# Edge counts of a graph adjacency matrix: one mask and two comparisons for four chunks of edges in place of two comparisons for each chunk

## The chip, the cores and the metric

The kernel runs on one core of a Trainium2 chip. The metric is the device time of one execution in microseconds (us), as the median of several executions. TensorE multiplies matrices, VectorE, ScalarE and GpSimd work elementwise, and SyncE issues DMAs. Each engine has a queue (a sequencer) that also executes register, branch and semaphore instructions in order and hands the others to the engine's data path.

## The reference, cut to what matters

A graph has 3125 nodes with 256 features and 100000 edges, sorted by destination. The destinations are `3125 * uniform ** 2`, so that low node numbers have many edges and high ones few. A chain of graph layers follows: four GCN layers, a graph-attention branch beside a state-space (Mamba) branch, three relational layers over eight edge types, and a last attention layer.

```python
x = normal(3125, 256); src = randint(100000, 0, 3125)
dst = minimum((3125 * uniform(100000) ** 2.0).astype(int32), 49999)
src, dst = both in the stable order of argsort(dst)
agg = segment_sum(norm[:, None] * h[src], dst)        # GCN
attn = exp_e / (segment_sum(exp_e, dst)[dst] + 1e-16)  # attention
```

The kernel works for GCN and attention from a dense matrix: entry (s, d) is the number of edges from node s to node d. The change is in the stage that makes this matrix.

## The kernel before

Nodes are padded to 3200, 25 tiles of 128. The edges are cut into 782 chunks of 128, one edge on each partition. The program runs stage by stage, with a barrier of all engines between stages: `constants`, `edge_tables`, `adjacency`, `load_x`, and then the layers.

`edge_tables` (lines 125 to 267) loads sources, destinations and types, turns them on TensorE so that a chunk is a column, and makes two keys for each edge: `key_lo`, which is (destination / 16) * 128 + source % 128, and `key_hi`, which is 16 * (source / 128) + destination % 16. It sends the smallest and largest destination of every chunk through DRAM, and works out for each of 200 groups of 16 destinations the first chunk that touches it, how many chunks do, and how many steps come before.

`adjacency` (lines 285 to 461) makes the matrix column by column. For each group n, VectorE walks over its chunks (line 321). For each chunk it writes `low` (128 x 128, line 325), which is 1 where the edge belongs to the group and its source modulo 128 is the column, and `high` (128 x 400, line 327), which is 1 at the column of its source tile and its destination in the group. TensorE multiplies the two (line 357) and accumulates the group's 128 x 400 counts in one of four PSUM banks. A ring of four slots (`RING`) lies between the engines: VectorE waits on `s_used`, TensorE on `s_hot`. The first chunk's product opens the bank (`start=True`), a product with zeros closes it (line 364), and ScalarE copies it to `counts` (line 416). After eight groups a tile is complete: ScalarE casts it (line 424), and in the next tile's groups 1 to 5 TensorE turns it (line 370, 25 products) and sums degrees (lines 375 and 377, 25 and 8 products), while ScalarE writes a mask of absent edges (line 407) and SyncE stores counts, cast strip and mask. A group has at least two steps, so that the first can stand outside the loop.

At each group, VectorE's and TensorE's queues call `group_of` (line 2489), which loads two registers from `g.groups`, one of them holding two numbers that are taken apart by `% 1024` and `// 1024`. `span_of` (line 270) is the like of it for the relational layers, with three loads.

## Time and profile before

| | |
|---|---|
| median of 3 executions | 9598.99 us (9585.42 to 9602.02) |
| the profiled execution, its time | 9601.42 us |
| its span in the trace | 9599.7 us |
| adjacency, first comparison to last product | 59.3 to 1396.5 us |
| steps in it, groups in it | 984, 200 |

A page of the profile shows the busy time of each engine, the span in 40 equal slices (here 240 us each) in tenths, the DMA queues and the costliest groups of instructions. Queries of the trace give the same for a stretch, a line or a tile, the waits, and the instructions in order of time. Names such as DVE are the engines': PE is TensorE's products, PEld its weight loads, DVE VectorE, ACT ScalarE, POOL GpSimd, SPq SyncE's queue; a q behind any name means the queue. Idle time put down to "issue" is time in which the data path waited for nothing but its own queue.

### The profile page before, as it was taken

The page shows a single profiled execution, that of the slowest core. Times are in us where ns is not written, and L with a number is a line of the kernel's source. Part 1 is how long each engine was busy: PE and PEld are TensorE (multiplying, and loading weights), DVE is VectorE, ACT ScalarE, POOL GpSimd, SP SyncE. Part 2 cuts the span into 40 slices and gives each one's busy share as a digit, 9 for nine tenths or more (in the row PEclk, how much of TensorE's full clock was granted, in tenths as well). Part 3 has the DMA queues.
Part 4 walks back from the last instruction along what each step waited for, and adds up shares of the span by engine and source line. Part 5 has one row for each costly group of instructions (what it writes and reads, how often), then busy time and mean ns, then how long its engine had stood idle before and what let it go on. Part 6 is the DMA issues. An engine that isn't in the chain of part 4 may idle for free. (4 is left out here: it accounts for less than half of the span.)

```text
span 9599.7 us, 112171 instructions
## 1 busy us (share of the span) xinstructions
PE 5887.8 (61%) x17649; PEld 2850.3 (30%) x17651; DVE 5067.8 (53%) x10613; ACT 1592.7 (17%) x2777; POOL 4423.1 (46%) x3713
## 2 busy tenths in 40 slices
PE   3444446621666633334489889888898888850453
PEld 1111116510222211113343444434444334430111
DVE  5443335659999958982333322233322333327896
ACT  0112221100444422112300000100011000010342
POOL 0000000030677716761027766576765777740793
PEclk5555557765899956667795677756777556665897
DMA  0112235532222220002243444433444333343333
GB/s 18 41 59 78 72 116 204 202 135 86 87 73 72 74 82 1 1 28 81 85 156 105 121 124 130 135 105 118 125 131 129 106 108 111 112 124 105 115 105 103
DMA packets 566945, 951.06 MB, mean 99 GB/s; under 512 B 78123, under 2 KB 441492, under 8 KB 564472
## 3 DMA queue, kind: packets, MB, share of 16 engines
q1 hardware_dynamic: 358280, 480.94, 15.7%
q0 software_dynamic: 142720, 403.03, 14.2%
q10 hardware_dynamic: 65888, 66.44, 2.1%
q8 instruction: 22, 0.36, 0.0%
q14 instruction: 35, 0.29, 0.0%
HBM read 718.07 MB, written 232.06 MB: 99 GB/s over the span
## 5 line engine op out<-in xcount | busy, mean ns | idle before, releaser
L2263 POOL DMA_INDIRECT rel1s_rows<-rel_table,rel1s_at x876 | 829.6, 947 | 393.5 <-DVE rel1s_at L2249 221.7
L2263 POOL DMA_INDIRECT rel0s_rows<-rel_table,rel0s_at x876 | 829.1, 946 | 370.6 <-DVE rel0s_at L2249 194.5
L2278 PE MATMUL rel2s_acc<-rel2s_rows,rel2s_hot 128*128 128x256 f32 x1752 | 879.7, 617 | 158.3 <-DMA rel2s_rows<-rel_table,rel2s_at 87.6
L2263 POOL DMA_INDIRECT rel2s_rows<-rel_table,rel2s_at x876 | 830.4, 948 | 302.4 <-issue 124.8
L357 PE MATMUL adj_acc<-adj_high,adj_low 128*128 x984 | 474.4, 487 | 711.3 <-DVE adj_high L327 706.2
L1371 PE MATMUL gatx_acc<-gatx_w,gatx_feat 128*65 128x400 f32 x1600 | 664.7, 569 | 338.3 <-DVE gatx_w L1293 296.2
L2278 PE MATMUL rel0s_acc<-rel0s_rows,rel0s_hot 128*128 128x256 f32 x1752 | 784.1, 565 | 127.0 <-DMA rel0s_rows<-rel_table,rel0s_at 72.1
L2278 PE MATMUL rel1s_acc<-rel1s_rows,rel1s_hot 128*128 128x256 f32 x1752 | 773.2, 557 | 135.0 <-DMA rel1s_rows<-rel_table,rel1s_at 78.1
L1283 DVE SCALAR_TENSOR_TENSOR gatx_w<-gatx_t,gatx_s 128x400 f32 (+1 forms) x800 | 745.9, 990 | 1.2 <-ACT gatx_t L1324 1.2
L325 DVE TENSOR_SCALAR adj_low<-g_numbers,g_offsets,g_key_lo 128x128 f16 x984 | 309.6, 315 | 801.7 <-issue 793.9
L1033 POOL IOTA rankk_owni<- 128x25 int32 x1 | 0.2, 159 | 1435.6 <-POOLq L72 1435.6
L1391 POOL TENSOR_SCALAR gatx_w<-gatx_w 128x400 f32<-128x400 f32 (+1 forms) x200 | 431.0, 2155 | 457.8 <-ACT gatx_w L1330 457.8
L2251 DVE TENSOR_SCALAR rel0s_hot<-g_numbers,g_dsts 128x128 f32 x876 | 290.5, 332 | 648.2 <-PE rel0s_acc L2278 630.6
L2251 DVE TENSOR_SCALAR rel1s_hot<-g_numbers,g_dsts 128x128 f32 x876 | 290.4, 332 | 643.3 <-PE rel1s_acc L2278 625.5
L2251 DVE TENSOR_SCALAR rel2s_hot<-g_numbers,g_dsts 128x128 f32 x876 | 297.7, 342 | 605.9 <-PE rel2s_acc L2278 599.5
L2278 PEld LDWEIGHTS rel2s_acc<-rel2s_rows,rel2s_hot 128*128 128x128 f32 x1752 | 412.6, 282 | 621.5 <-DVE rel2s_hot L2251 310.8
L2278 PEld LDWEIGHTS rel0s_acc<-rel0s_rows,rel0s_hot 128*128 128x128 f32 x1752 | 381.4, 258 | 521.8 <-DVE rel0s_hot L2251 231.1
L2278 PEld LDWEIGHTS rel1s_acc<-rel1s_rows,rel1s_hot 128*128 128x128 f32 x1752 | 376.0, 254 | 523.8 <-DVE rel1s_hot L2251 250.4
L1330 ACT ACTIVATE gatx_w<-gatx_w,gatx_s 128x400 f32<-128x400 f32 x800 | 437.1, 617 | 519.4 <-DVE gatx_w L1283 519.4
L1371 PE MATMUL latx_acc<-latx_w,latx_feat 128*65 128x400 f32 x800 | 307.4, 507 | 267.0 <-POOL latx_w L1393 267.0
L1846 PE MATMUL mamb_acc<-mamb_hc,g_ident 128*128 128x512 f32 x420 | 237.0, 731 | 381.6 <-DVE mamb_hc L1837 381.6
L1371 PEld LDWEIGHTS gatx_acc<-gatx_w,gatx_feat 128*65 128x65 f32 x1600 | 234.1, 155 | 765.5 <-DVE gatx_w L1293 411.7
(478 smaller groups left out, 9670.1 us busy)
## 6 DMA issues: line engine op xcount, KB each, us to landing
agg_strip<-strips SPq DMA_DIRECT2D x100, 800.0 KB, 6.0
adj<-adj_counts SPq DMA_DIRECT2D x25, 1600.0 KB, 7.1
gatx_adj<-adj SPq DMA_DIRECT2D x200, 200.0 KB, 2.4
latx_adj<-adj SPq DMA_DIRECT2D x200, 200.0 KB, 2.3
gatx_feat<-local_rows SPq DMA_DIRECT2D x200, 130.0 KB, 2.3
rel_table<-rel0p_res POOLq DMA_DIRECT2D x25, 1024.0 KB, 5.1
rel_table<-rel0s_prod ACTq DMA_DIRECT2D x25, 1024.0 KB, 4.9
rel_table<-rel1s_prod ACTq DMA_DIRECT2D x25, 1024.0 KB, 5.0
```

Of the source, the lines that this page charges most:

```text
L325: nc.vector.tensor_scalar(low[:, bass.ds(slot, 1), :].rearrange("p a d -> p (a d)"), base[:, 0:P], g.offsets[:, bass.ds(n, 1)], g.key_lo[: ...
L357: nc.tensor.matmul(bank[:, 0:W16], low[:, bass.ds(slot, 1), :].rearrange("p a d -> p (a d)"), high[:, bass.ds(slot, 1), :].rearrange("p a ...
L1033: nc.gpsimd.iota(owni[:, :], [[P, T]], base=-HALF, channel_multiplier=1).then_inc(s_io, 1)
L1283: last = nc.vector.scalar_tensor_tensor(w[u][:, h, :], t1[:, h, bass.ds(c, J)], s08[:, bass.ds(s, 1), h], t2[:, h, bass.ds(c, J)], ALU.add ...
L1330: last = nc.scalar.activation(w[u][:, h, :], w[u][:, h, :], ACT.Exp, bias=s02[:, bass.ds(s, 1), h])
L1371: last = nc.tensor.matmul(acc[k][h][:, :], feat[u][:, h * 65:(h + 1) * 65], w[u][:, h, :], start=False, stop=False)
L1391: nc.gpsimd.tensor_scalar(mine, mine, 1.0, None, ALU.min).then_inc(s_pm, 1)
L1846: last = nc.tensor.matmul(acc[:, a:b], ident[:, :], hc[:, a:b], start=False, stop=False)
L2251: nc.vector.tensor_scalar(hot[u][:, :], g.numbers[:, bass.ds(t * P, P)], g.dsts[:, bass.ds(c0 + u, 1)], None, ALU.is_equal).then_inc(s_hot, 1)
L2263: pool.indirect_dma_start(rows[u][:, :], None, table, bass.IndirectOffsetOnAxis(ap=at[u][:, 0:1], axis=0)).then_inc(s_in[u], 16)
L2278: nc.tensor.matmul(acc[:, :], hot[u][:, :], rows[u][:, :], start=False, stop=False).then_inc(s_used, 1)
```

## The change

Four chunks make one step, a batch (`Q = 4`), and a group has one batch or more. The constants hold every number four times in a row, so that the four chunks of a batch are the innermost dimension of one instruction. Each edge now has three 16-bit keys: source modulo 128 (`key_lo`), the column of `high` plus 1 (`key_hi`), and the destination group (`key_group`). In a batch VectorE makes `mine` (128 x 4), which is `key_hi` where the edge is of this group and 0 elsewhere, then `low` for four chunks (128 x 128 x 4) and, after a wait for `mine`, `high` for four chunks (128 x 400 x 4), both by TENSOR_TENSOR. TensorE makes four products from operands whose elements stand four apart. The ring has two slots of a batch in place of four of a chunk. A bank is opened by a product with zeros. The three numbers of a group lie side by side, and one load instruction brings them into three registers; they need no division. `edge_tables` takes the keys from the turned numbers with integer operations, and turns three arrays, not four. `spans` gets the same layout, but `span_of` keeps its three loads.

```diff
-RING = 4
+RING = 2
+Q = 4
@@ edge_tables, VectorE
-            nc.vector.tensor_scalar(bits[:, 0], raw[:, 1], 3, ~(P - 1), ALU.logical_shift_left, ALU.bitwise_and)
...
-            nc.vector.tensor_tensor(keys[:, 0], bits[:, 0], bits[:, 1], ALU.add)
-            nc.vector.tensor_tensor(keys[:, 1], bits[:, 2], bits[:, 3], ALU.add)
+            dve.wait_ge(s_T, 3)
+            nc.vector.tensor_copy(ints[:, 0, :], psum[0][:, 0:W])
+            v(nc.vector.tensor_copy(ints[:, 1, :], psum[1][:, 0:W]))
...
+            nc.vector.tensor_copy(g.key_lo[:, :], bits[:, 0, :])
+            nc.vector.scalar_tensor_tensor(g.key_hi[:, :], bits[:, 1, :], 1.0, bits[:, 2, :], ALU.add, ALU.add)
+            nc.vector.tensor_copy(g.key_group[:, :], bits[:, 3, :])
...
-            nc.vector.tensor_scalar(count, count, 2.0, None, ALU.max)
+            whole(count, Q)
@@ adjacency, VectorE
+            dve.wait_ge(s_io, 1)
+            nc.vector.tensor_copy(num1[:, :, :], numi[:, :, :])
+            nc.vector.tensor_scalar(num0[:, :, :], numi[:, 0:P, :], -1.0, None, ALU.add).then_inc(s_num, 1)
+            dve.wait_ge(s_num, 1)
                 with dve.Fori(0, count, 1) as j:
-                    c = step_start(nc, first + j)
+                    c = step_start(nc, first + j * Q)
                     slot = dve.snap((before + j) % RING)
                     dve.wait_ge(s_used, before + j + 1)
-                    nc.vector.tensor_scalar(low[:, bass.ds(slot, 1), :].rearrange("p a d -> p (a d)"), base[:, 0:P],
-                                            g.offsets[:, bass.ds(n, 1)], g.key_lo[:, bass.ds(c, 1)], ALU.add, ALU.is_equal)
-                    nc.vector.tensor_scalar(high[:, bass.ds(slot, 1), :].rearrange("p a d -> p (a d)"), base,
-                                            g.key_hi[:, bass.ds(c, 1)], None, ALU.is_equal).then_inc(s_hot, 1)
+                    nc.vector.scalar_tensor_tensor(slot_of(mine, slot).rearrange("p a q -> p (a q)"), g.key_group[:, bass.ds(c, Q)],
+                                                   g.group_number[:, bass.ds(n, 1)], g.key_hi[:, bass.ds(c, Q)],
+                                                   ALU.is_equal, ALU.mult).then_inc(s_mine, 1)
+                    nc.vector.tensor_tensor(slot_of(low, slot).rearrange("p a n q -> p (a n) q"), num0[:, :, :],
+                                            g.key_lo[:, bass.ds(c, Q)].unsqueeze(1).to_broadcast([P, P, Q]), ALU.is_equal)
+                    dve.wait_ge(s_mine, before + j + 1)
+                    nc.vector.tensor_tensor(slot_of(high, slot).rearrange("p a n q -> p (a n) q"), num1[:, :, :],
+                                            slot_of(mine, slot).to_broadcast([P, W16, Q]), ALU.is_equal).then_inc(s_hot, 1)
@@ adjacency, GpSimd
+            nc.gpsimd.iota(numi[:, :, :], [[1, W16], [0, Q]], base=1, channel_multiplier=0).then_inc(s_io, 1)
@@ adjacency, TensorE
-                pe.wait_ge(s_copied, n + 1)
-                visit(0, True)
-                with pe.Fori(1, count, 1) as j:
-                    visit(j, False)
+                pe.wait_ge(s_copied, n + 1)
+                nc.tensor.matmul(bank[:, 0:W16], g.zeros[:, 0:P], g.zeros[:, 0:W16], start=True, stop=False)
+                with pe.Fori(0, count, 1) as j:
+                    slot = pe.snap((before + j) % RING)
+                    pe.wait_ge(s_hot, before + j + 1)
+                    for i in range(Q):
+                        last = nc.tensor.matmul(bank[:, 0:W16], low[:, bass.ds(slot, 1), :, i].rearrange("p a n -> p (a n)"),
+                                                high[:, bass.ds(slot, 1), :, i].rearrange("p a n -> p (a n)"),
+                                                start=False, stop=False)
+                    last.then_inc(s_used, 1)
@@ three registers in one load
+def three_of(nc, eng, table, n, regs, least, most, last):
+    eng.reg_load(regs, table[0:1, bass.ds(n, 1), :].rearrange("o n k -> o (n k)"))
+    first, count, before = (eng.snap(r) for r in regs)
...
-    both = eng.value_load(g.groups[0:1, 0, bass.ds(n, 1)], min_val=2 * 1024, max_val=C * 1024 + C - 1)
-    before = eng.value_load(g.groups[0:1, 1, bass.ds(n, 1)], min_val=0, max_val=NG * C)
-    return both % 1024, eng.snap(both // 1024), before
+    return three_of(nc, eng, g.groups, n, regs, 1, most, NG * most)
```

## Rows read from the trace of the kernel before

**Rows 1.** The page: the span in 40 slices of 240 us.
```profile
PEclk5555557765899956667795677756777556665897
...
GB/s 18 41 59 78 72 116 204 202 135 86 87 73 72 74 82 1 1 28 81 85 156 105 121 124 130 135 105 118 125 131 129 106 108 111 112 124 105 115 105 103
```

**Rows 2.** Stretch: length; busy PE, PEld, DVE, ACT, POOL; clock, DMA share, GB/s.
```profile
112.90:1399.00 1286.10, 599.84 (x2520) 216.64 (x2518) 506.43 (x1854) 255.41 (x321) 0.00 (x0) 0.52 0.18 61
```

**Rows 3.** Waits from 57 to 1408 us: total, times, longest.
```profile
DVE adj_low L325 <- issue: 793.9, 964, 3.7
PE adj_acc L357 <- DVE adj_high L327: 706.2, 914, 3.7
...
DVE adj_low L325 <- PE adj_acc L357: 7.8, 20, 0.4
```

**Rows 4.** VectorE in order of time: start, duration; two steps and a group's end between.
```profile
1101.81 0.32 DVE L325 TENSOR_SCALAR adj_low<-g_numbers,g_offsets,g_key_lo 128x128 f16 x1 [0.39 <-issue]
...
1104.69 0.32 DVE L325 TENSOR_SCALAR adj_low<-g_numbers,g_offsets,g_key_lo 128x128 f16 x1 [2.33 <-issue]
...
1105.63 0.32 DVE L325 TENSOR_SCALAR adj_low<-g_numbers,g_offsets,g_key_lo 128x128 f16 x1 [0.40 <-issue]
```

**Rows 5.** VectorE's queue by line: duration in ns, minimum, median, maximum.
```profile
L325 DVEq FUSED_REGOPS  x1968: 62/118/230, 58.9 to 1395.2; - x197
...
L2492 DVEq FUSED_REGOPS  x400: 65/130/190, 58.0 to 1393.6; - x134
...
L2492 DVEq TENSOR_LOAD <-g_groups x200: 299/303/992, 58.1 to 1393.2; - x100
```

**Rows 6.** TensorE's queue: weight loads in order of time, then instructions by line.
```profile
1391.72 0.15 PEld L357 LDWEIGHTS adj_acc<-adj_high,adj_low 128*128 x1 [0.18 <-issue]
...
1392.32 0.10 PEld L357 LDWEIGHTS adj_acc<-adj_high,adj_low 128*128 x1 [0.45 <-issue]
...
L2491 PEldq FUSED_REGOPS  x380: 42/157/171, 57.5 to 1393.1; - x190
...
L2491 PEldq TENSOR_LOAD <-g_groups x200: 296/303/976, 57.0 to 1392.8; - x100
...
L357 PEldq ALU_OP  x984: 32/36/36, 60.1 to 1396.1; - x197
```

**Rows 7.** TensorE in order of time: turning, and the two degree sums.
```profile
1388.77 0.81 PE L375 MATMUL adj_ind<-g_ones,adj_strip 128*128 128x1 bf16 x25
...
1389.43 2.83 PE L377 MATMUL adj_deg<-adj_strip,g_ident 128*128 128x400 bf16 x8
...
1400.09 1.89 PE L370 MATMUL adj_tp<-g_ident,adj_strip 128*128 128x128 bf16 x16 [3.47 <-ACT adj_strip L424]
```

**Rows 8.** Two VectorE lines with one tensor input: minimum, median, maximum ns.
```profile
L120 DVE CAST g_numbers<-const_num x1: 1827/1827/1827, 5.5 to 5.5; 128x3200 f16<-128x3200 int32 x1
...
L1073 DVE TENSOR_SCALAR rank_before<-g_numbers,rank_own x25: 1046/1053/1055, 1529.8 to 1833.2; 128x3200 bf16<-128x3200 f16 x25
```

**Rows 9.** The stages before adjacency, in order of time.
```profile
2.43 2.80 POOL L114 IOTA const_num<- 128x3200 int32 x1
...
21.14 1.09 DVE L221 TENSOR_TENSOR edge_keys<-edge_bits 128x896 f32<-128x896 int32 x1
22.15 1.08 DVE L222 TENSOR_TENSOR edge_keys<-edge_bits 128x896 f32<-128x896 int32 x1
...
24.68 0.27 DVE L227 COPY edge_endsT<-edge_t 14x128 f32<-14x128 f32 x1
...
31.95 0.63 DVE L236 TENSOR_SCALAR edge_tmp<-edge_row,edge_edge 100x782 f32<-100x782 f32 x1 [0.70 <-DMA edge_row<-ends_rows]
...
55.92 0.16 DVE L266 CAST g_spans<-edge_tiles 1x25 int32<-1x25 f32 x1
56.00 0.16 DVE L267 CAST g_spans<-edge_tiles 1x25 int32<-1x25 f32 x1
```

More of the change, by code:

```diff
@@ L264, in _ @@
-            nc.vector.tensor_tensor(g.spans[:, 2, 0:T], total_t, steps_t, ALU.subtract)
-            nc.vector.scalar_tensor_tensor(g.groups[:, 0, :], count, 1024.0, first, ALU.mult, ALU.add)
-            nc.vector.tensor_copy(g.spans[:, 0, 0:T], first_t)
-            nc.vector.tensor_copy(g.spans[:, 1, 0:T], steps_t)
+            nc.vector.tensor_copy(g.groups[:, :, 0], first)
+            nc.vector.tensor_copy(g.groups[:, :, 1], count)
+            nc.vector.tensor_tensor(g.groups[:, :, 2], total, count, ALU.subtract)
@@ L270, in span_of @@
+            nc.vector.tensor_copy(g.spans[:, :, 0], first_t)
+            nc.vector.tensor_copy(g.spans[:, :, 1], steps_t)
+            nc.vector.tensor_tensor(g.spans[:, :, 2], total_t, steps_t, ALU.subtract)
 def span_of(eng, g, t, size):
-    k, K = SPANS.index(size), len(SPANS)
     most = -(-C // size)
-    first = eng.value_load(g.spans[0:1, 0, bass.ds(t, 1)], min_val=0, max_val=C - 1)
-    count = eng.value_load(g.spans[0:1, 1 + k, bass.ds(t, 1)], min_val=2 if size == G_SUM else 1, max_val=most)
@@ L276, in span_of @@
-    before = eng.value_load(g.spans[0:1, 1 + K + k, bass.ds(t, 1)], min_val=0, max_val=T * most)
+    first = eng.value_load(g.spans[0:1, bass.ds(t, 1), 0], min_val=0, max_val=C - 1)
+    count = eng.value_load(g.spans[0:1, bass.ds(t, 1), 1], min_val=LEAST, max_val=most)
+    before = eng.value_load(g.spans[0:1, bass.ds(t, 1), 2], min_val=0, max_val=T * most)
     return first, count, before
@@ L345, in _ @@
             pe.sem_inc(s_used, RING)
+            regs = three_registers(pe, "group")
             pe.sem_inc(s_copied, 4)
@@ L2486, in row_number, with three_registers, group_of @@
     return nc.vector.scalar_tensor_tensor(out, kind, float(NP), src, ALU.mult, ALU.add)
[L2489 to L2493 removed]
+def three_registers(eng, name):
+    return [eng.alloc_register(f"{name}{k}") for k in range(3)]
+def three_of(nc, eng, table, n, regs, least, most, last):
+    eng.reg_load(regs, table[0:1, bass.ds(n, 1), :].rearrange("o n k -> o (n k)"))
+    why = "made by edge_tables within these bounds"
+    first, count, before = (eng.snap(r) for r in regs)
+    return (nc.s_assert_within(first, 0, C - 1, skip_runtime_bounds_check_because=why),
+            nc.s_assert_within(count, least, most, skip_runtime_bounds_check_because=why),
+            nc.s_assert_within(before, 0, last, skip_runtime_bounds_check_because=why))
+def group_of(nc, eng, g, n, regs):
+    most = -(-C // Q)
+    return three_of(nc, eng, g.groups, n, regs, 1, most, NG * most)
 def program(nc, x, src, dst, kind, noise, gcn, local, ssm, mix, rel, last, out):
```

129 lines of the change are left out of this document (64 added, 65 removed).

## The prediction

> **What bounds the kernel now.** The page comes first. The program runs stage by stage, and the stage that changes, adjacency, fills the first five and a half slices, with TensorE's clock granted at 0.5 and DMA far below what later slices move [rows 1]. The busy times of the stretch say that no data path is the bound there: TensorE is busy 600 of 1286 us, VectorE 506, ScalarE 255, DMA 18% [rows 2]. The waits say who holds up whom. TensorE waits 706 us for `adj_high`, 914 times; VectorE waits for TensorE 20 times, 7.8 us in all; and VectorE's own idle time, 794 us, is put down to its queue [rows 3]. VectorE in order of time gives the prices. A step lasts 0.94 us, though its two comparisons end 0.55 us after the first begins; where a group ends, the next step starts 2.88 us after the last, so a group costs 1.94 us beside its steps [rows 4]. With 984 steps and 200 groups that is 984 x 0.94 + 200 x 1.94 = 1313 us, and the stage measures 1337 us (59.3 to 1396.5), 2% more. So the stage is bound by register and branch work in VectorE's queue. Every later stage stands behind the barrier at its end, and what the stage gains comes off the span whole.
>
> **How many steps are left.** I took the chunks that each group touches from the reference's sorted destinations. The sum of max(2, chunks) over 200 groups is 984, the count in the trace; the sum of ceil(chunks / 4) is 299. There are 135 groups of one batch, 52 of two and 13 of three to 15. So 200 first batches come with a group's cost and 99 without. Four per batch is almost nowhere full: 1196 products replace 984, since short groups multiply empty chunks.
>
> **VectorE's queue.** A batch has the old step's work and one instruction more, with register addresses for `mine`, `key_group` and `key_hi`, and one more wait. The nearest rows are the register instructions of line 325, 0.118 us each [rows 5]; two of these with their gaps make 0.36, so 1.30 us for a batch. Bounds: 0.94 (nothing more) and 1.5. A group loses one load (0.303), two register instructions (0.130 each) and the division, with gaps some 0.8 of its 1.94 us [rows 5], and gains three copies between registers; I take 1.25, between 1.1 and 1.45. First batches: 200 x 2.55 = 510 us.
>
> **VectorE's data path.** No row shows a TENSOR_TENSOR with only 16-bit operands. The 4-byte one of 896 elements starts 1.01 us before its successor, that is 0.93 at one element a cycle of 1.04 ns and 0.08 more [rows 9]. For one input, going from a 4-byte to a 2-byte source takes 3200 elements from 1.83 to 1.05 us [rows 8]. I apply that halving: `low` (512) 0.35, `high` (1600) 0.91, `mine` 0.08 like the small instructions that start 0.08 apart [rows 9]. That is 1.34, with 0.1 for the wait 1.45 us, longer than the queue's 1.30, and it sets the 99 further batches: 144 us. In first batches it lies beside the queue's 2.55 us. VectorE together: 510 + 144 = 654 us. If the halving does not hold, the batch is 0.08 + 0.61 + 1.75 = 2.44 us, and with the wait 2.54: 200 x 2.6 + 99 x 2.54 = 771 us. The Trainium skill ("VectorE: DVE Perf Modes", "The perf-mode tier table") says that tensor_tensor runs at two elements a cycle for 16-bit data in SBUF and at one for fp32; by it the sum is the 654, and by the 4-byte row alone the 771; no run here shows yet which.
>
> **TensorE's data path.** Eight 400-column products last 2.83 us, of which a product's own tail is counted once: 0.333 us each at the granted 0.5 [rows 2, 7]. 1196 of them are 398 us; 200 openers with zeros 67; 200 closers some 20; and for each of 25 tiles the turning (25 of which 16 last 1.89 us, so 2.95) and the degree sums (0.81 and 2.83), 6.6 us, are 165 [rows 7]. Together 650 us. Opening by zeros costs 67 us of data path and takes a bank's start out of the loop; before, TensorE was waiting anyway.
>
> **TensorE's queue.** Two steps whose inputs were ready stand 0.60 us apart [rows 6]. Three more products add address arithmetic (two register instructions of 0.032) and dispatch; with gaps 0.23 each, between 0.15 and 0.33. Batch: 1.3 us (1.05 to 1.6). A group had two loads at 0.303 with some 0.16 of register work and a check after each [rows 6], about 1.7 us; one less leaves 1.1 with opener and closer. 299 x 1.3 + 200 x 1.1 + 25 x 2.4 for the tile's other instructions = 669 us.
>
> **The sum.** 654, 650 and 669 us are three resources of one load, joined by two slots. In most tiles eight groups take 21 us on each, but TensorE's comes in lumps (3.6 us of degree sums in one group, longer than a group's 2.55 us). Before, with the others half idle, the excess over the sum was 2%; I take 12% over the largest: 750 us. 1337 - 750 = 587 us less.
>
> **Around it.** In `edge_tables` four bit operations and two sums leave the path ahead of `edge_ends` going to DRAM (that transfer holds the spans from 24.68 to 31.95 us [rows 9]); the transfer starts some 4 us earlier, but two copies, the bit operations and three key instructions now stand before the spans on VectorE, some 8 us from the turned numbers on: 1 us earlier in all. `whole` adds three dependent instructions, and the layouts two: 1 us later. In adjacency, the iota of 1600 numbers (half of the 2.80 us of line 114 [rows 9]) and two casts (half of 1.83 [rows 8] and less) come before the first batch: 3 us. Net 3 us. `span_of` keeps three loads in 75 tiles, where only an address changes: 0, at most 2 us. Stores: 82 MB in 750 us are 109 GB/s, against 204 in a later slice [rows 1], so they stay hidden; without that cover a tile would wait for the store two before it. ScalarE's 255 us hide in 750.
>
> The profiled execution took 9601.4 us; 9601.4 - 587 + 3 = 9017, and the median stands 2.4 below it: **9015 us**.
>
> **Rivals.**
> - *VectorE at one element a cycle* (13%). 771 us and 8% for handover, 830 us: 9095. For it: no row with two 16-bit tensors; against: the halving in [rows 8]. A broadcast operand with rows of four elements could also prevent it.
> - *Dearer queues* (15%). Every strided slice gets its own address arithmetic: 1.6 us a batch and 1.3 a group on TensorE, 478 + 260 + 60 = 798, with 6% 845: 9110. For it: queues, not data paths, set the pace before [rows 3].
> - *A faster clock* (8%). With TensorE busy 85% and not 47% [rows 2], 2.4 GHz might be granted; the later stages with a clock of 0.8 and more are in [rows 1]. Then the queues decide: 690 us, 8955.
> - *The ring serialises* (4%). If two slots let no work overlap, 654 + 650 = 1304 us: 9569. Against: VectorE needs a slot only two batches later.
> - *TensorE reads at half speed* (7%). Both operands now have a stride of four elements. At 0.667 us a product: 798 + 252 = 1050, with 12% 1180 us: 9445.
> - *TensorE reads at a quarter* (3%), the one on the other side. 1196 x 1.333 + 252 = 1846 us, 509 more: 10111. It decides from (1337 - 252) / 1196 = 0.91 us a product on. Every TensorE row of before reads whole runs, the degree sums runs of 16 elements [rows 7], so nothing excludes it. The Trainium skill ("Advanced Engine Details and Errata", "Memory Cachelines") says that SBUF gives full performance from two hits on a 16-byte line and less where each access opens another; four fp16 numbers apart are exactly two hits, so by it nothing is lost here, and with eight chunks in a batch it would be; no run here shows it.
>
> **How the numbers follow.** The forecast has 50%, the rivals 13, 15, 8, 4, 7 and 3. The low end is the queues' sum with no excess at a fast clock, 640 us (8905). The high end takes the slow comparison and the dear queues together, 905 us (9170). In between lie the forecast and three rivals, 86%. A measurement here tells a change from none at 0.2%, 19 us: faster 0.95, within 0.01, slower 0.04.
>
> **What would show it.** In the changed profile: 299 of `adj_high`; `high` at 0.9 to 1.1 us (at 1.8 the halving failed); successive further batches 1.45 us apart; 2.55 us between groups of one batch; products 0.333 us apart in fours (wider: the stride, or the queue if the data path idles between). VectorE's wait for TensorE should grow from 7.8 us to the order of 100. Wrong would be: a product over 0.4 us, first batches over 3 us apart, or a stage after adjacency whose length changes.

## The result, and the profile after

The changed kernel takes 10330.93 us, median of 4 executions (10314.73 to 10334.56), against 9597.4 us for the kernel before (4 executions, 9585.42 to 9602.02). The ratio is 1.0763 (1.0744 to 1.0782). It is 733 us slower, where 9015 us and a gain of 587 us were forecast. The prediction has the wrong sign, and its range (8905 to 9170) does not hold the time.

Three parts of the page of the changed kernel: the slices, now of 258 us, two DMA queues (packets, MB, share), and two groups of products.

```profile
span 10332.9 us, 111704 instructions
...
PEclk7875567777657988566698667776677656665797
...
GB/s 43 105 136 158 137 128 134 133 133 143 122 99 86 73 73 70 71 1 1 64 59 152 117 115 127 130 133 105 117 127 131 119 107 109 112 120 119 108 105 103
...
q1 hardware_dynamic: 372680, 562.87, 16.8%
...
q10 hardware_dynamic: 146528, 125.42, 3.9%
...
L675 PE MATMUL agg_acc<-agg_split,agg_strip 128*128 128x192 bf16 (+1 forms) x5000 | 648.4, 307 | 472.8 <-DMA agg_strip<-strips 472.7
...
L379 PE MATMUL adj_acc<-adj_high,adj_low 128*128 x1196 | 462.9, 531 | 53.9 <-DVE adj_high L342 41.1
```

The slices show two things. The clock in the first three is 0.7 to 0.8, where it was 0.5 [rows 1], and the two slices of over 200 GB/s that stood behind adjacency [rows 1] are gone: six slices of 128 to 143 GB/s, the fifth to the tenth, stand in their place. The last two rows name the two kinds of products. The 1196 of adjacency are there as forecast. The 5000 of line 675 are the aggregation of the GCN layers, which no line of the diff touches, and they waited 472.7 us for strips from DRAM.

Stretches of the changed kernel (columns as in [rows 2]): adjacency, `load_x`, and the aggregation.

```profile
65.00:836.00 771.00, 633.53 (x2986) 271.25 (x2987) 451.13 (x896) 250.72 (x319) 0.00 (x0) 0.77 0.29 102
848.00:1310.00 462.00, 21.01 (x626) 18.70 (x626) 228.25 (x133) 1.51 (x2) 0.16 (x1) 0.50 0.49 147
1390.00:2600.00 1210.00, 660.71 (x5213) 605.76 (x5214) 262.03 (x135) 35.64 (x104) 0.00 (x0) 0.77 0.39 137
```

Adjacency is nearly as short as forecast: 771 us, where 750 were forecast, against 1337. The loss comes behind it. Two single lines show it: the instructions of one line, with count, duration in ns (minimum, median, maximum) and first and last start. First the changed kernel.

```profile
L805 DVE TENSOR_TENSOR loadx_low<-loadx_counts,loadx_high x25: 3491/3493/3493, 871.8 to 1300.0; 128x3200 bf16<-128x3200 f32 x25
...
L675 PE MATMUL agg_acc<-agg_split,agg_strip x5000: 245/296/373, 1396.8 to 2587.1; 128*128 128x192 bf16 x97, 128*128 128x195 bf16 x96
its engine sat idle before it (us, times) until:
  DMA agg_strip<-strips: 968.9, 201
```

The same two in the kernel before, whose lines 786 and 656 they are.

```profile
L786 DVE TENSOR_TENSOR loadx_low<-loadx_counts,loadx_high x1: 3493/3493/3493, 1432.1 to 1432.1; 128x3200 bf16<-128x3200 f32 x1
...
L656 PE MATMUL agg_acc<-agg_split,agg_strip x2500: 245/247/373, 1531.9 to 1845.3; 128*128 128x192 bf16 x97, 128*128 128x195 bf16 x96
its engine sat idle before it (us, times) until:
  issue: 0.7, 4
```

The counts are what matters here, not the durations: 25 rounds in place of 1, and 5000 products in place of 2500. A round or a product is the same instruction as before. The 968.9 us of waiting are those of the products and of their weight loads together; the products' own are the 472.7 of the page. Twice the products take 3.8 times as long (1190.3 us against 313.4). One wait of SyncE's queue, which issues the loads of strips, says why (total, times, longest):

```profile
SPq L657 <- PE agg_acc L675: 908.7, 100, 16.0
```

Both strips of a tile go to the same buffer, one after the other. SyncE issues loads in order and waits at each second strip until TensorE is through with the first, 100 times and 908.7 us in all; a strip then needs 4.5 us (median) from issue to landing. With one strip a tile TensorE waited for none. No run changed the buffers, so this is read from the trace and the code. The whole difference can be added up from these starts:

| stretch | before | after | difference |
|---|---|---|---|
| start of the program to adjacency's last product | 1396.2 | 835.9 | -560 |
| last product to first `loadx_low` | 35.9 | 35.9 | 0 |
| first to last `loadx_low` | 0 | 428.2 | +428 |
| last `loadx_low` to first product of the aggregation | 99.8 | 96.8 | -3 |
| first to last product of the aggregation | 313.4 | 1190.3 | +877 |
| sum | | | +742 |

The spans differ by 10332.9 - 9599.7 = 733 us, so the later stages give 9 back.

What decides the counts stands at the end of `adjacency`, in lines that the diff only moves (349 to 356 after, 334 to 341 before); the waits between them and the semaphore counts are left out here:

```python
nc.vector.tensor_reduce(most[0:1, :], acc[0][0:1, 0:P], AX.X, ALU.max)
...
nc.vector.tensor_scalar(most[0:1, :], most[0:1, :], 256.0, 1.0, ALU.is_ge, ALU.add)
...
nc.vector.tensor_scalar(g.strips_before[:, :], g.numbers[0:1, 0:32], float(HALF), most[0:1, 0:1], ALU.add, ALU.mult)
nc.vector.tensor_scalar(g.low_tiles[:, :], most[0:1, 0:1], float(T - 1), float(T - 2), ALU.mult, ALU.subtract)
```

`most` is the largest out-degree of a node, as the matrix has it. From 256 on the kernel no longer relies on a bf16 number to hold a count exactly, and each tile gets a second strip with what the first may have lost: `low_tiles` goes from 1 to 25 rounds, and the aggregation takes two strips a tile. The 100000 edges are 781 chunks of 128 and 32 edges. The last chunk with edges is filled up with 96 padding edges from node 3199 to node 3199 (the `memset` of `raw` with `PAD`), and what lies beyond is padding alone. Before, the last group has one chunk with edges and takes the least number of steps, two: 96 + 128 = 224 padding edges on node 3199. After, its one batch reads four chunks: 96 + 3 * 128 = 480. That is over 256, and the program chooses the long way, though the entry (3199, 3199) belongs to no node of the graph.

### The profile page after: what moved, and what is told of

Same layout as the page of the kernel before. It is cut to its first block and busy times, and to the rows that moved or that the text cites. A ratio compares the mean times of both kernels' runs of the same rounds, so it can differ in the third digit from the quotient of the medians.

```text
span 10332.9 us, 111704 instructions
## 1 busy us (share of the span) xinstructions
PE 6338.5 (61%) x21155; PEld 3289.5 (32%) x21156; DVE 5166.5 (50%) x9671; ACT 1589.3 (15%) x2775; POOL 4431.7 (43%) x3714
## 5 line engine op out<-in xcount | busy, mean ns | idle before, releaser
L675 PE MATMUL agg_acc<-agg_split,agg_strip 128*128 128x192 bf16 (+1 forms) x5000 | 648.4, 307 | 472.8 <-DMA agg_strip<-strips 472.7
L675 PEld LDWEIGHTS agg_acc<-agg_split,agg_strip 128*128 128x128 bf16 x5000 | 579.1, 124 | 523.8 <-DMA agg_strip<-strips 496.2
```

Source lines behind the costliest of these rows:

```text
L675: last = nc.tensor.matmul(acc[u][:, 0:W], strip[u][:, s * P:(s + 1) * P], split[:, s, :], start=False, stop=False)
```

## Experiments

The theory (padding): the 480 padding edges set the second strip, and the rest of the change brings what was forecast. Its rival: the later stages are slower for something else that the change does to them, such as the layout of `spans`, the place of the strips or the clock. Once this was settled, the runs went to adjacency: which of its prices bounds it now.

Every kernel below that loads three numbers at once also holds them in registers of their own (three register instructions more in `three_of`, 0.07 us a group on VectorE's queue); this is not shown again. With it the last product of adjacency comes at 847.8, 849.9 and 846.4 us in experiments 1, 2 and 4, against 835.9 in the changed kernel. The kernel before took 10150.8 us on the chip of experiments 1 to 4, 10164.0 us on that of 5 to 8, and 9600.65 us on that of 9 to 12, so whole times are not compared across chips. Adjacency itself is compared by its last product: the kernel before has it at 1396.2 us on the chip of the prediction, and the same adjacency in experiment 3 at 1396.5 on the slower chip of experiments 1 to 4. The other two chips have no trace of it.

**1 and 2. The limit just at and just above 480.** Only the constant of the comparison is changed.

```diff
-            nc.vector.tensor_scalar(most[0:1, :], most[0:1, :], 256.0, 1.0, ALU.is_ge, ALU.add).then_inc(s_v, 1)
+            nc.vector.tensor_scalar(most[0:1, :], most[0:1, :], 480.0, 1.0, ALU.is_ge, ALU.add).then_inc(s_v, 1)
```

> The changed kernel; the comparison behind the stage takes two strips per tile from a largest out-degree of 480 on, where it took them from 256. Each of the three loaded numbers is also held at 0 or more by a register instruction, as in every later run on the changed kernel. Theory A (padding): a group's last batch reads up to three chunks past the 782 of the edge list, each 128 padding edges from node 3199 to node 3199, so that node's out-degree is 96 + 3 x 128 = 480 and the flag stays set: about 10330 us as the changed kernel, load_x with 25 rounds and 200 strip loads, and the register instructions worth 0 to 20 us. Theory B (the counts of real nodes are too high, for example a bank not cleared by its opener): also 10330 us, since whatever value crossed 256 may exceed 480. Theory C (the largest degree lies between 256 and 479 for another reason): one strip, about 9040 us.

> The changed kernel with the comparison from 481 on. Theory A: the largest out-degree is 480 exactly, so the flag is not set; load_x goes back to one round (32 us in place of 462) and the aggregations to 100 strip loads. What the changed kernel lost behind adjacency is its 733 us plus the 561 us that adjacency ended earlier, 1294 us; so 10331 - 1294 = 9037 us, up to 9060 with the register instructions, ratio 0.942 to 0.944. Theory B: no change, 10330 us. Theory D (a large part of what is lost behind adjacency is not the second strip but contention or a lower clock): between 9100 and 10000 us.

Measured: with 480 one execution took 10892.19 us, 741 above before on that chip, and the line of `loadx_low` has its 25 rounds. With 481 it took 9593.58 us, ratio 0.9455 (0.944 to 0.9469), and the rounds are one. Lines 805 and 675 with the limit at 481:

```profile
L805 DVE TENSOR_TENSOR loadx_low<-loadx_counts,loadx_high x1: 3492/3492/3492, 885.9 to 885.9; 128x3200 bf16<-128x3200 f32 x1
...
L675 PE MATMUL agg_acc<-agg_split,agg_strip x2500: 245/246/373, 985.5 to 1299.9; 128*128 128x192 bf16 x97, 128*128 128x195 bf16 x96
```

One unit of the constant is worth 1299 us, and everything else of the change is in both kernels. So the largest out-degree is 480, exactly the number of padding edges, and the rival is out: with the short way, 2500 products take 314 us, as before.

**3. The kernel before, with the limit at 224.**

```diff
-            nc.vector.tensor_scalar(most[0:1, :], most[0:1, :], 256.0, 1.0, ALU.is_ge, ALU.add).then_inc(s_v, 1)
+            nc.vector.tensor_scalar(most[0:1, :], most[0:1, :], 224.0, 1.0, ALU.is_ge, ALU.add).then_inc(s_v, 1)
```

> The kernel before with the comparison from 224 on in place of 256. Theory A: in the kernel before the last group has two steps of one chunk, 96 + 128 = 224 padding edges, just under the limit; so now the flag is set and the time rises by the same 1294 us to 10891 us (10860 to 10920), ratio about 1.135. Theory B: real out-degrees (32 on average) are the largest in the kernel before, no change, 9597 us. Theory D: a rise of less than 1294 us, since the old adjacency stage comes before it.

Measured: 11456.84 us, ratio 1.1281 (1.126 to 1.1302), 1306 us more. Its line 656:

```profile
L656 PE MATMUL agg_acc<-agg_split,agg_strip x5000: 245/290/373, 1957.0 to 3146.9; 128*128 128x192 bf16 x97, 128*128 128x195 bf16 x96
```

The old adjacency with the second strip: 5000 products in 1190 us, the same as in the changed kernel. The kernel before thus reached at least 224, and stayed on the short way by 32 edges at most. The price of the long way does not depend on the change.

**4. The cause taken away: padding with a destination outside the matrix.** The padding edges get destination 3200, which no group owns, so that the limit can stay at 256.

```diff
-            nc.gpsimd.memset(raw[:, :, R, :], PAD).then_inc(s_fill, 1)
+            for k, pad in enumerate((PAD, NP, PAD)):
+                nc.gpsimd.memset(raw[:, k, R, :], pad).then_inc(s_fill, 1)
...
-            sp.wait_ge(s_fill, 1)
+            sp.wait_ge(s_fill, 3)
```

> The changed kernel with padding edges given destination 3200, which no group of 16 nodes and no tile owns (source 3199 and the comparison from 256 stay). Theory A: no padding edge is counted, the flag is not set, 9037 to 9060 us, the same as with the limit at 481, and the output stays the reference's. Theory B: 10330 us. Theory D: as there.

Measured: 9587.0 us, ratio 0.945 (0.9437 to 0.9463), the same as experiment 2 by another way. This is the change as it was meant, and it beats both kernels. What it would take on the chip of the prediction can only be estimated: by the ratio, 0.945 x 9597.4 = 9070 us; by the difference, 9597.4 - 563.8 = 9034 us, which fits better with a stage that lasts as long on both chips. That is 19 to 55 above the forecast of 9015 and inside its range. The experiments from 5 to 10, and 12, are built on this version.

**5. Products that read whole runs.** Since a product reads every fourth element of both operands, it was open what the stride costs (two rivals of the prediction). Here each product takes one contiguous quarter of the batch; the counts are then other numbers, and the number, sizes and order of the products stay. The limit of the second strip is put at 1e9 here, so that the later stages keep one strip whatever the counts are (not shown again).

```diff
-                        last = nc.tensor.matmul(bank[:, 0:W16], low[:, bass.ds(slot, 1), :, i].rearrange("p a n -> p (a n)"),
-                                                high[:, bass.ds(slot, 1), :, i].rearrange("p a n -> p (a n)"),
+                        last = nc.tensor.matmul(bank[:, 0:W16], low[:, bass.ds(slot, 1)].rearrange("p a n q -> p (a n q)")[:, i * P:(i + 1) * P],
+                                                high[:, bass.ds(slot, 1)].rearrange("p a n q -> p (a n q)")[:, i * W16:(i + 1) * W16],
```

> As e4, but each of a batch's four products reads a quarter of the slot as one run (128 and 400 elements side by side) in place of every fourth element. The counts are therefore those of other edges, and the comparison that decides on a second strip is put out of reach so that the later stages keep one. Only adjacency is read. In the changed kernel the four products of a batch start 0.353 us apart although the granted clock is 0.77 and the 400-column products with the identity, which read 32-byte runs, start 0.17 us apart. Theory S (the stride sets the pace): 0.17 us apart where the clock is 2.4 GHz and 0.333 where it is 1.2; adjacency from 778 us to about 690, now held by VectorE. Theory Q (address arithmetic and dispatch in TensorE's queue set the pace): 0.35 us apart as before, adjacency unchanged at 770 to 785 us.

Measured: one execution took 9568.6 us. TensorE in order of time (start, duration), first the changed kernel with one batch of a group, then this one.

```profile
506.20 0.33 PE L374 MATMUL adj_acc<-g_zeros 128*128 128x400 bf16 x1
506.48 1.58 PE L379 MATMUL adj_acc<-adj_high,adj_low 128*128 x4
507.88 0.19 PE L383 MATMUL adj_acc<-g_zeros 128*128 128x1 bf16 x1
```

```profile
504.68 0.34 PE L375 MATMUL adj_acc<-g_zeros 128*128 128x400 bf16 x1 [0.99 <-ACT adj_counts L436]
505.16 0.84 PE L380 MATMUL adj_acc<-adj_high,adj_low 128*128 x4
505.87 0.17 PE L384 MATMUL adj_acc<-g_zeros 128*128 128x1 bf16 x1
```

Four products last 0.84 us in place of 1.58. By the starts of single products (medians from the second to the fourth of a batch), contiguous ones stand 0.168 us apart at the clock of 2.4 GHz and 0.333 at 1.2, and strided ones 0.355 at either. So the stride costs a factor of 2.1 at the high clock and next to nothing at the low one, and the price is real. Yet the stage got only 29 us shorter (last product at 817.7 in place of 846.4), where 90 were expected. Its stretch:

```profile
65.00:818.00 753.00, 506.01 (x2987) 253.14 (x2987) 450.04 (x897) 251.15 (x319) 0.00 (x0) 0.83 0.30 105
```

TensorE is busy 506 us and not 634, so 128 us of data path went for a gain of 29. The waits of this kernel say who holds the pace: three rows.

```profile
DVE adj_mine L337 <- issue: 249.4, 181, 3.0
...
PE adj_acc L375 <- ACT adj_counts L436: 80.5, 89, 1.5
...
DVE adj_mine L337 <- PE adj_acc L380: 53.6, 40, 3.1
```

VectorE's wait for its own queue is longer than its wait for TensorE, and the banks' opener waits 80.5 us for ScalarE's copies. The expectation failed in its size: TensorE's data path was not the bound. Even the 29 us are not all the products': 17 of them are loads of `g_groups` that lasted less in this one execution (the table behind experiment 12).

**6. A ring of four batches.**

```diff
-RING = 2
+RING = 4
```

> As e4 with four slots of a batch in place of two. In e4 VectorE waits 132 us for a slot, 104 times. Theory R (the two slots cost what the three equal loads lose to each other): most of that wait goes, adjacency from 778 to 700 to 730 us, the whole 50 to 75 us faster than e4, ratio 0.937 to 0.940. Theory P (TensorE itself is the bound, 634 of 771 us busy): the wait moves elsewhere, adjacency not under 760 us, ratio 0.943 to 0.945.

Measured: 9575.84 us, ratio 0.9415 (0.9401 to 0.9429) against 0.945 (0.9437 to 0.9463) in experiment 4. In the trace the last product is at 819.0, 27 us earlier. VectorE still waits 116.0 us for TensorE, 94 times (131.8 and 104 times in experiment 4). That lies between the two expectations (50 to 75 us, and next to nothing): the coupling by two slots costs some 27 of the 780 us, and 23 of these are in the 99 further batches of groups, which stand 1.39 us apart (median) in place of 1.52.

**7 and 8. Batches of two and of eight.** `Q` is 2, then 8; the stride is 4 and 16 bytes.

```diff
-Q = 4
+Q = 8
```

> As e4 with two chunks in a batch: 546 batches and 1092 products in place of 299 and 1196, elements two apart (4 bytes). VectorE: 200 groups at 2.4 us with their first batch and 346 further ones at 1.1 us give 860 us, so adjacency about 880, 100 us more than e4, ratio 0.954 to 0.957. Theory S: with a stride of 4 bytes more of a line is used, products under 0.3 us apart at the high clock. Theory S' (any stride halves the rate): 0.35 us apart.

> As e4 with eight chunks in a batch: 222 batches but 1776 products, elements eight apart (16 bytes). Theory S with a price for each line touched: the products are 0.7 us apart, 1776 x 0.7 = 1240 us and the rest, adjacency 1400 us or more, the whole slower than e4 by 650. Theory S': as at four apart, 0.35 us, 1776 x 0.353 = 627 us and some 250 for the rest, adjacency 880 to 950 us.

Measured: with two 9823.23 us, ratio 0.9666 (0.9652 to 0.9681), last product at 1072.6, later than expected; with eight one execution took 10290.83 us against 10164.0 for before, last product at 1538.1. The stretch of adjacency and one batch of the kernel with eight:

```profile
65.00:1538.00 1473.00, 1469.50 (x3565) 403.78 (x3566) 584.08 (x666) 253.47 (x319) 0.00 (x0) 0.52 0.16 53
```

```profile
505.77 5.86 PE L380 MATMUL adj_acc<-adj_high,adj_low 128*128 x8
```

Eight products of 400 columns last 5.86 us: 0.710 us apart, twice as long as at eight bytes. TensorE is busy the whole 1473 us, so here its data path is the only bound, and batches of eight lose to the kernel before. With two, the two products of a batch start 0.176 us apart at 2.4 GHz and 0.290 at 1.2, and the first two of a contiguous batch in experiment 5 stand 0.168 and 0.287 apart. So a stride of four bytes costs next to nothing, and the stage is longer for other reasons, which no run takes apart: it has 546 batches, each with the queue's price, its granted clock is back at 0.54, and TensorE and VectorE wait for each other (210.7 and 282.6 us). Four is the best of the three sizes. The stretch with two:

```profile
65.00:1073.00 1008.00, 666.25 (x2881) 261.77 (x2881) 539.59 (x1632) 253.19 (x319) 0.00 (x0) 0.54 0.24 78
```

**9 and 10. The load of three numbers, undone in two ways.** In 9 the group's numbers are packed and loaded as before, with two loads and the division; in 10 they are loaded by three single loads.

```diff
-    return three_of(nc, eng, g.groups, n, regs, 1, most, NG * most)
+    both = eng.value_load(g.groups[0:1, 0, bass.ds(n, 1)], min_val=1024, max_val=C * 1024 + C - 1)
+    before = eng.value_load(g.groups[0:1, 1, bass.ds(n, 1)], min_val=0, max_val=NG * C)
+    return both % 1024, eng.snap(both // 1024), before
```

> As e4, with the two loads of one number each and the division of the kernel before in place of the load of three. In the changed kernel the load of three lasts 0.758 us on VectorE's queue at the median and 255 us in 200 groups, since some last up to 2.9 us; before, two loads of 0.307 lasted 151 us with such excesses. Theory M (the median path decides): from the group's first register instruction to the loop's 1.58 us before and 1.10 now, so 0.48 x 200 = 96 us more: adjacency 870 us, ratio 0.953 to 0.956. Theory X (the long loads weigh as much): 75 us of excess go, so within 25 us of e4, ratio 0.944 to 0.948.

```diff
-    return three_of(nc, eng, g.groups, n, regs, 1, most, NG * most)
+    first = eng.value_load(g.groups[0:1, bass.ds(n, 1), 0], min_val=0, max_val=C - 1)
+    count = eng.value_load(g.groups[0:1, bass.ds(n, 1), 1], min_val=1, max_val=most)
+    before = eng.value_load(g.groups[0:1, bass.ds(n, 1), 2], min_val=0, max_val=NG * most)
+    return first, count, before
```

> As e4, with three loads of one number each, every one followed by register work and a check as in span_of. Some 0.53 us for each, 1.6 us where e4 has 1.10, so by theory M 100 us more, ratio 0.953 to 0.956; by theory X 75 us of excess less, 0.945 to 0.948. If three loads take clearly less than one load of three, the ratio is under 0.944.

Measured: 9096.6 us with two packed loads, ratio 0.9472 (0.946 to 0.9485), last product at 886.5, 40 us later than in experiment 4 and 51 later than in the changed kernel, whose three numbers are not held; 9226.83 us with three, ratio 0.9613 (0.96 to 0.9626), last product at 1033.5, 187 later. The load instructions on VectorE's queue, first of the changed kernel, then of the kernel with three loads.

```profile
L2515 DVEq TENSOR_LOAD <-g_groups x200: 740/758/2906, 62.8 to 830.2; - x100
```

```profile
L2525 DVEq TENSOR_LOAD <-g_groups x200: 287/293/982, 63.0 to 1023.7; - x100
```

One load of three numbers has a median of 0.758 us and a sum of 254 us; three loads of one have 0.293 each and a sum of 252. So a load is paid mostly by its numbers: 0.12 us of the three are saved by the one instruction. The rest of what it saves stood around the single ones: the address before, and the register work and a check of the value at run time after each, which the load of three leaves out. For one of the three loads, on VectorE's queue:

```profile
L2525 DVEq FUSED_REGOPS  x200: 204/204/224, 63.6 to 1024.5; - x100
L2525 DVEq SEQ_ASSERT  x200: 23/23/33, 63.8 to 1024.7; - x100
```

No run keeps the load of three and its checks, so how much of the gain is the missing checks stays open. By the starts of `mine`, from one group to the next (median), experiment 4 needs 2.54 us, experiment 9 2.90 and experiment 10 3.58. For 10 that is 199 x 1.04 = 207 us more, less 27 us of long loads, where the last product is 187 us later. For 9 it is 199 x 0.36 = 72 us more, less 48 us of long loads and plus 15 us of other waits, where the last product is 40 us later. So of the two expectations of experiment 9 each had a part: the path through the queue is dearer at the median, and the long loads weigh about as much.

**11. The load of three alone, in the kernel before.** `groups` gets the new layout and `group_of` the one load; steps, ring and comparisons stay.

```diff
-    both = eng.value_load(g.groups[0:1, 0, bass.ds(n, 1)], min_val=2 * 1024, max_val=C * 1024 + C - 1)
-    before = eng.value_load(g.groups[0:1, 1, bass.ds(n, 1)], min_val=0, max_val=NG * C)
-    return both % 1024, eng.snap(both // 1024), before
+    return three_of(nc, eng, g.groups, n, regs, 2, C, NG * C)
```

> The kernel before with one part of the change alone: the three numbers of a group side by side and brought by one load (with the register instruction that holds each at 0 or more), batches, keys and openers as before. Theory M: 0.48 us less in each of 200 groups, 96 us less, ratio 0.990 to 0.992. Theory X: up to 75 us of long loads given back, ratio 0.996 to 1.000. Padding edges still reach 224 and no second strip is taken.

Measured: 9472.55 us, ratio 0.9865 (0.985 to 0.988), last product at 1269.1 in place of 1396.2. This part alone brings 127 us, 31 more than expected. By VectorE's starts half of it is not the load: the 199 changes of group give 63 us (median 2.47 in place of 2.88, less 17 us of longer loads), and the 784 further steps, which load nothing, give 64, as they last 0.858 us in place of 0.937. The loop's own instructions show part of it, first before, then here:

```profile
L321 DVEq FUSED_REGOPS  x1968: 58/78/93, 58.8 to 1395.5; - x197
```

```profile
L323 DVEq FUSED_REGOPS  x984: 58/58/66, 59.3 to 1267.9; - x197
L323 DVEq ALU_OP  x984: 47/47/58, 59.9 to 1268.5; - x197
```

The end of a step has a register instruction of 0.093 us before and of 0.047 here. The kernel before hands on `both % 1024` as an expression and not in a register of its own. That the steps pay for this is argued; experiment 9, which goes back to it, again has 0.091 us there, where experiment 4 has 0.047. In the changed kernel the same part brings 40 us, not 127: there are 99 further batches, which it does not shorten, and the one load's long cases cost 48 us more than those of two loads.

**12. Two packed loads and a ring of four.**

> e6 (four slots, padding edges counted nowhere) with the two loads of e9 in place of the load of three. Theory M: 0.951 to 0.954. Theory X: 0.941 to 0.945.

Measured: 9071.05 us, ratio 0.9452 (0.9439 to 0.9465), last product at 859.8, 27 us earlier than in experiment 9. The ring gives the same 27 us with either way of loading, so the two parts add up. No kernel that counts the right edges has a lower ratio than experiment 6.

**Where VectorE's time goes.** Starts of the first instruction of each step or batch (`low` before and in 11, `mine` in the others), worked out from the kept traces, in us. A change of group is the distance that holds a group's loads. A load is long here where the loads of a group last over 1.3 times their median; the excess is what lies above the median.

| kernel | change of group, median | 199 changes | excess of long loads | same changes, over the median | further steps or batches |
|---|---|---|---|---|---|
| before | 2.88 | 600 | 28 | 28 | 784 x 0.94 = 736 |
| 11, load of three in before | 2.47 | 536 | 44 | 44 | 784 x 0.86 = 672 |
| changed | 2.47 | 602 | 104 | 103 | 99, 166 |
| 4 | 2.54 | 612 | 103 | 103 | 99, 165 |
| 5, contiguous | 2.54 | 591 | 85 | 85 | 99, 159 |
| 6, ring of four | 2.52 | 605 | 103 | 103 | 99, 142 |
| 9, two packed loads | 2.90 | 651 | 54 | 54 | 99, 165 |

A long load delays the next group by what it is long, to the microsecond, in every kernel. In the changed kernel 199 x 2.47 = 491 us, 103 of long loads, 166 of further batches and 8 of other waits make the 768 us from the first batch to the last. So VectorE's queue is still the bound at the changes of group, though some of its waits there are put down to TensorE, and TensorE costs it time mostly in the further batches.

## Why the prediction was wrong, point by point

**What bounds the kernel.** Right: with the load of three alone the stage shortens by 127 us, in the steps as well as between the groups (experiment 11), so register work in VectorE's queue held it. Wrong is its last sentence, "Every later stage stands behind the barrier at its end, and what the stage gains comes off the span whole". That took the later stages' lengths as fixed. They depend on a number that the changed stage makes.

**How many steps are left: the step that failed.** The counts are right, 299 batches and 1196 products. But the sentence "short groups multiply empty chunks" was not true of all: chunks beyond a group's own hold other groups' edges, which the mask removes, except for the last group, whose padding edges are its own. It counts 480 of them, and 224 before. Experiments 1 to 4 show it: 1299 us hang on the 480, and without them the change has a ratio of 0.945. No rival held it, though everything was there to read: the `memset` of `raw`, the comparison with 256 at the end of the stage, and loops in `load_x` and the aggregation that are bounded by a number from memory. The last clause of the prediction named the sign ("a stage after adjacency whose length changes"), but had no price and no chance.

**VectorE's queue.** 2.55 us for a group of one batch was forecast; the 199 changes of group have a median of 2.47. Two groups in order of time:

```profile
506.75 0.22 DVE L336 SCALAR_TENSOR_TENSOR adj_mine<-g_key_group,g_group_number,g_key_hi  x1 [0.84 <-PE adj_acc L379]
...
509.20 0.22 DVE L336 SCALAR_TENSOR_TENSOR adj_mine<-g_key_group,g_group_number,g_key_hi  x1 [0.98 <-issue]
```

**VectorE's data path.** 1.45 us was forecast for a further batch. Where no slot is waited for it is 1.39 to 1.42, and 1.39 is the median with a ring of four (experiment 6); the median of the 99 in the changed kernel is 1.52. The three instructions of one batch and the start of the next:

```profile
101.26 0.22 DVE L336 SCALAR_TENSOR_TENSOR adj_mine<-g_key_group,g_group_number,g_key_hi  x1 [0.89 <-PE adj_acc L379]
101.40 0.42 DVE L339 TENSOR_TENSOR adj_low<-adj_num,g_key_lo 128x512 f16 x1
101.74 0.98 DVE L342 TENSOR_TENSOR adj_high<-adj_num,adj_mine 128x1600 f16 x1
102.68 0.22 DVE L336 SCALAR_TENSOR_TENSOR adj_mine<-g_key_group,g_group_number,g_key_hi  x1
```

By the starts, `mine` takes 0.14 us, `low` 0.34 and `high` 0.94 for 1600 elements, where 0.08, 0.35 and 0.91 were forecast. The halving taken from the one-input rows holds for two inputs, with the broadcast operand too, and the rival of one element a cycle is out. The Trainium skill ("VectorE: DVE Perf Modes", "The perf-mode tier table") says two elements a cycle for such data, and the trace agrees: 0.94 us for the 1600 elements of `high`, where one element a cycle was forecast at 1.75.

**TensorE's data path.** 0.333 us a product was forecast and 0.355 measured, 7% more, so 1196 products make 425 us and not 398. The number is nearly right, but for a reason that the prediction did not have: at 0.333 it was the low clock's price, and the clock did rise, from 0.52 [rows 2] to 0.77. The stride took back what the clock gave. So the rival of a faster clock was right in its condition and wrong in its gain, and the rival of half speed had its factor at the high clock, not on top of the low one's. Here the Trainium skill ("Advanced Engine Details and Errata", "Memory Cachelines") and the measurement differ. By it, two hits on a 16-byte line lose nothing; at 2.4 GHz the product with two hits takes 0.355 us, the contiguous one 0.168, and the one with four hits 0.176 (experiments 5 and 7): four hits are enough, two are not. The measurement decides. That one hit to a line costs more than two, which the section also says, the trace bears out: 0.711 us.

**TensorE's queue.** 2.4 us for a group of one batch was forecast; the products of two such groups start at 506.48 and 508.84, 2.36 us apart, and the second did not wait for VectorE, whose `high` began at 507.24 and lasted 0.98.

**The sum.** 750 us was forecast for the stage and 771 measured, 2.8% more. The 12% for handover came out as 15% over the largest of the three forecasts (669). That the number fits is in part luck, for the excess is mostly something else. It was put down to three equal loads that lose time to each other; by the table above, VectorE's queue alone fills the stage, and the term missing from its 654 us is the 104 us of long loads, which the prediction put at nothing. What a ring of four takes away, 27 us, is the handover. VectorE waits 128.8 us for TensorE, where the order of 100 was named:

```profile
DVE adj_mine L336 <- issue: 191.0, 118, 3.0
DVE adj_mine L336 <- PE adj_acc L379: 128.8, 105, 3.1
...
PE adj_acc L379 <- DVE adj_high L342: 41.1, 50, 7.9
```

What was mis-sized is one piece of the group's cost: a load of three was taken to save a whole load, and costs 0.758 us against two of 0.303. It still came out near the forecast of 1.25 us a group, because the work around the loads that goes with it, the checks of the values among it, was worth more than I had counted (experiments 9 to 11).

**Around it.** The first batch comes 5.4 us later than the first comparison did (64.7 against 59.3), where 3 were forecast; the iota of 1600 numbers takes 4.79 us, more than the 2.80 us of 3200 numbers that I halved [rows 9]. Each value stands four times in a row, and half the elements were not half the price. No engine waits for a store, as forecast, and they run at 102 GB/s in the stage; but they are not without a price if they are what makes the loads of `g_groups` long (last section).

**What stays open.** In the repaired kernel the stage takes 780 us; a contiguous read takes 29 off and a deeper ring 27, and neither was tried with the other. With the deeper ring the table leaves nothing to TensorE or ScalarE: 199 changes at 2.52 us of queue work, 103 us of long loads and 99 further batches at VectorE's own 1.39 us. What makes the loads long, and how much of the load of three's gain is the checks that it leaves out, no run has tested.

## What to carry to other kernels

Before costing a stage, ask what it computes that later stages branch on or loop over, and what the new form puts into that number. Where a loop is coarsened, its last unit reads past the data: follow the padding through to the result, since here 256 padding edges more on a node that does not exist cost 1300 us, and moving them outside (one constant) turned 7.6% slower into 5.5% faster (on another chip). When the loading of numbers is changed, look at the steps that only use them: in experiment 11 they gave half of the gain. When an operand of TensorE is interleaved to make VectorE's instructions longer, price the stride at the clock that the stage will then have, and try the interleaving at more than one width.

## What the runs showed of the hardware

A product of 400 columns, both operands 16-bit, by the stride of its elements; medians from start to start at each granted clock:

| stride | 16-byte stretches passed | 1.2 GHz | 2.4 GHz |
|---|---|---|---|
| 2 bytes (contiguous), second to fourth | 50 | 0.333 us | 0.168 us |
| 2 bytes, first of a batch | 50 | 0.287 | 0.168 |
| 4 bytes (batches of two), first of a batch | 100 | 0.290 | 0.176 |
| 8 bytes (batches of four), second to fourth | 200 | 0.356 | 0.355 |
| 16 bytes (batches of eight) | 400 | 0.711 | 0.711 |

In the last three rows at 2.4 GHz the time goes by the bytes that 400 columns pass over, 1.76 to 1.78 ns for each 16. These strides cannot show how large the unit is that is paid for; a wider stride would. At 1.2 GHz the columns are dearer up to a stride of four bytes, the bytes passed from eight on, and from there the clock does not show. Both operands were strided together in every run, so the table does not say which of them is paid for. The kernel before has no product with operands strided like this, so its trace could not show the price.

TensorE was busy 1469.5 of 1473 us in the kernel with batches of eight, and its granted clock stayed at 0.52; with batches of four it was busy 634 of 771 us at 0.77, and with contiguous products 506 of 753 us at 0.83. So busy time as the trace counts it did not by itself bring the higher clock: with batches of eight TensorE spent its time on reads that were slow.

A load of registers from SBUF takes 0.29 to 0.31 us for one number and 0.758 for three (medians on VectorE's queue), and some take three times as long and more: up to 2.906 us for three numbers and 0.992 for one. In the changed kernel 67 of VectorE's 200 loads last over one and a half times the median. Each of the 67 begins within 6 us of the issue of a tile's store (counts, strip or mask; the loads of 202.6 and 238.5 us follow issues of 202.0 and 237.9), and while they last the 16 DMA engines are busy 93% of the time on average, against 1% in the other 133. In the kernel before it is 46 of 400 loads, with 95% against under 1% in the others. The excess over the median adds up to 104 us in the changed kernel and 29 in the kernel before, and it lies on the path in full. That the stores' traffic is the cause is argued from this coincidence; no run took the stores away or moved them.
